# A two-layer transformer block on one core: the first stage with a joined mask, an fp32 projection and a key-only norm, and a low part that moves to GpSimd

## What is computed

```python
def _layernorm(x, axis=-1, eps=1e-05):
    m = jnp.mean(x, axis=axis, keepdims=True)
    v = jnp.var(x, axis=axis, keepdims=True)
    return (x - m) / jnp.sqrt(v + eps)
...
        qkv = x @ Wqkv.T + bqkv
        q, k, v = jnp.split(qkv, 3, axis=-1)
        q = rmsnorm(q, gq)
        k = rmsnorm(k, gk)
...
        q = apply_rope(q, cos, sin)
        k = apply_rope(k, cos, sin)
        qf = jax.nn.relu(q)
        kf = jax.nn.relu(k)
        vpad = jnp.concatenate([v, jnp.ones_like(v[..., :1])], axis=-1)
        vk = jnp.einsum('bhlp,bhld->bhpd', vpad, kf)
        res = jnp.einsum('bhpd,bhld->bhlp', vk, qf)
        attn = res[..., :-1] / (res[..., -1:] + EPS_LIN)
...
    x = L0_attn_x
    xn = _layernorm(x, axis=-1)
    x = x + _L0_attn_ref(xn, ...) + _L0_ffn_ref(xn, ...)
    xn = _layernorm(x, axis=-1)
    x = x + _L1_attn_ref(xn, ...) + _L1_ffn_ref(xn, ...)
```

## Time and profile before

| | |
|---|---|
| median of 3 runs | 414.53 us (414.43 to 414.73) |
| the profiled execution | 415.73 us, its span 413.9 us, mean granted TensorE clock 0.942 |
| VectorE busy | 361.8 us, 87% of the span |
| TensorE busy | 323.3 us, 78% |
| GpSimd busy | 235.4 us, 57% |
| ScalarE busy | 187.9 us, 45% |
| VectorE in the full step from 98.90 to 115.58 us | 15.42 of 16.68 us |
| TensorE, ScalarE, GpSimd in that step | 14.02, 11.67, 8.27 us |

### The profile page before, as it was taken

The page is one execution under the profiler, slowest core; times in us unless marked ns, Lnnn a source line. Parts: engine busy times, 40 slices in busy tenths (PEclk is TensorE's granted clock), DMA queues, the critical chain, the costliest instruction groups (busy, mean ns, idle before and its releaser), DMA issues.

```text
span 413.9 us, 5058 instructions
## 1 busy us (share of the span) xinstructions
PE 323.3 (78%) x1487; PEld 244.7 (59%) x1487; DVE 361.8 (87%) x815; ACT 187.9 (45%) x502; POOL 235.4 (57%) x149
## 2 busy tenths in 40 slices
PE   0357595887888877632409999999999999999995
PEld 0247485876777766621306666666666666666662
DVE  3786988999989975589999989999999999999791
ACT  2434546667766674630304262533526253352621
POOL 9061563634725522156345977879597787958450
PEclk9999888999999999695857999999999999999999
DMA  7720000101101002121000000000000000000000
GB/s 181 230 51 1 2 0 0 53 2 52 51 2 51 30 22 98 63 71 30 1 0 1 2 0 25 2 24 1 2 25 1 26 2 25 1 2 26 0 27 26
DMA packets 13248, 12.51 MB, mean 30 GB/s; under 512 B 1548, under 2 KB 9924, under 8 KB 13220
## 3 DMA queue, kind: packets, MB, share of 16 engines
q1 hardware_dynamic: 10944, 10.10, 7.7%
q0 software_dynamic: 736, 0.95, 1.1%
q10 hardware_dynamic: 1540, 1.12, 0.9%
HBM read 5.88 MB, written 2.10 MB: 19 GB/s over the span
## 4 chain that ended last, share of the span: by engine, by line
PE 42%; DVE 34%; issue 8%; POOL 6%; ACT 6%; DMA 1%; ACTq 1%; DVEq 0%; POOLq 0%
PE VK L840 14%; PE Q L840 12%; PE T L840 8%; PE ND L840 4%; ACT xn L555 4%; DVE mv L1105 3%; POOL prod_qk L780 3%; PE T L836 3%; DVE bst L1095 2%; POOL prod_pv L790 2%; DVE rope_a L1266 2%; DVE rope_b L1268 2%; PE Q L836 2%; DMA wout<-in_woutT 1%; DVE sgc L1466 1%
## 5 line engine op out<-in xcount | busy, mean ns | idle before, releaser
L790 POOL TENSOR_TENSOR prod_pv<-prob,qkv 128x1024 f32<-128x1024 f32 x32 | 69.6, 2212 | 45.0 <-DVE att L1383 24.2
L694 ACT ACTIVATE sg<-Q 128x512 f32<-128x512 f32 x72 | 43.1, 598 | 97.6 <-PE Q L840 94.9
L780 POOL TENSOR_TENSOR prod_qk<-qkv 128x1024 f32<-128x1024 f32 x32 | 75.9, 2402 | 16.7 <-DVE scr L1366 16.7
L840 PE MATMUL VK<-hid,w 128*128 128x512 f32 x144 | 74.5, 599 | 0.0
L840 PE MATMUL Q<-xT_hi,w_hi 128*128 128x512 f32 x72 | 52.3, 726 | 0.7 <-ACT combT L680 0.7
L1466 DVE TENSOR_TENSOR sgc<-ND,sg 128x512 f32<-128x512 f32 x64 | 43.7, 682 | 6.6 <-PE ND L840 4.6
L1479 DVE TENSOR_TENSOR hid<-T,sgc 128x512 f32<-128x512 f32 x64 | 43.6, 681 | 0.3
L840 PE MATMUL T<-xT_hi,w_hi 128*128 128x512 f32 x72 | 28.9, 401 | 17.1 <-DVE hid L1479 17.1
L743 POOL TENSOR_TENSOR mxy<-xn,amax 128x512 f32<-128x512 f32 x8 | 8.5, 1066 | 57.5 <-DVE amax L1250 57.5
L1366 DVE TENSOR_REDUCE scr<-prod_qk 128x128 f32<-128x1024 f32 x32 | 38.4, 1207 | 0.0
L1383 DVE TENSOR_REDUCE att<-prod_pv 128x128 f32<-128x1024 f32 x32 | 38.3, 1197 | 0.0
(11 more groups left out here) (202 smaller groups left out, 840.7 us busy)
## 6 DMA issues: line engine op xcount, KB each, us to landing
xT_hi<-xTs_hi SPq DMA_DIRECT2D x8, 256.0 KB, 2.3
xT_lo<-xTs_lo SPq DMA_DIRECT2D x8, 256.0 KB, 2.3
out_x<-fin SPq DMA_DIRECT2D x8, 256.0 KB, 2.3
x<-in_x SPq DMA_DIRECT2D x2, 256.0 KB, 5.0
wraw<-in_w1T SPq DMA_DIRECT2D x1, 512.0 KB, 10.8
w<-in_w2T SPq DMA_DIRECT2D x1, 512.0 KB, 5.1
wraw<-in_w3T ACTq DMA_DIRECT2D x1, 512.0 KB, 3.2
sel<-in_c_sel POOLq DMA_DIRECT2D x4, 128.0 KB, 2.8
```

Source lines behind the costliest of these rows:

```text
L694: act.activation(sg[:, side(half, s), :], QB[side(half, s)][:, :], ACT.Silu).then_inc(sg_ready, 1)
L780: pool.tensor_tensor(prod_qk[:, t % 2], bc(qkv2[:, TH * half + t, j, 0:D], 1, NB), qkv2[:, :, j, D:2 * D], ALU.mult).then_inc(qk_prod, 1)
L790: pool.tensor_tensor(prod_pv[:, t % 2].rearrange("p (h e) b -> p b h e", e=HD), bc(prob[:, t], 3, HD), qkv2[:, :, j, 2 * D:QKV].rearrange( ...
L840: return pe.matmul(o, lhsT, rhs, start=start, stop=stop)
```

## The change

It does eight things in the first part. (1) `v_ext` gets 16 columns of ones in place of one, and `headmask` and `headsel` become one mask of 144 columns, so that one product makes `vk_bd`. (2) The first projection is one fp32 product per tile; the hi and lo parts of the weights and of xnT are gone. (3) `features` scales and clips k alone (`kf`); q is transposed as it comes out of the rotary sum, and ScalarE's copy out of the bank is a relu. (4) As q is then without its norm's factor, `attention` adds the epsilon times the root in the denominator. (5) `ln_values` uses `bn_aggr` on each tile, and one addition of the epsilon. (6) ScalarE copies the second transposed tile twice, whole (`xTs`) and from there rounded (`xTs_hi`). (7) The low part of it is subtracted by GpSimd, between `mx_round` and `rope_add`. (8) `rope_add` also waits until the transposes of the chunk before have read `rope_ab`.

```diff
-            act.dma_start(headmask[:, :], d["c_headmask"]).then_inc(ld_const, 16)
-            act.dma_start(headsel[:, :], d["c_headsel"]).then_inc(ld_const, 16)
+            act.dma_start(headmask[:, 0:D], d["c_headmask"]).then_inc(ld_const, 16)
+            act.dma_start(headmask[:, D:D + H], d["c_headsel"]).then_inc(ld_const, 16)
...
-                act.activation(wqkv_hi[:, :], wqkv_raw[:, :], ACT.Copy).then_inc(wqkv_hi_ready, 1)
...
             def qfT_evac(c):
-                evac(qfT[:, :, :], tiles(T1), (qfT_ps, c + 1), [], qfT_ready)
+                act.wait_ge(qfT_ps, c + 1)
+                act.activation(qfT[:, :, :], tiles(T1), ACT.Relu).then_inc(qfT_ready, 1)
...
-                evac(xTs_hi[:, :, :], tiles(T1), (xn2T_ps, c + 1), [(xTs_free, c + 1)], xn2T_hi)
+                evac(xTs[:, :, :], tiles(T1), (xn2T_ps, c + 1), [(xn2T_lo, c)], xn2T_whole)
+                act.wait_ge(xn2T_whole, c + 1)
+                act.wait_ge(xTs_free, c + 1)
+                act.activation(xTs_hi[:, :, :], xTs[:, :, :], ACT.Copy).then_inc(xn2T_hi, 1)
...
             def rope_add(c):
                 pool.wait_ge(qkv_rope, NJ * c + NJ)
                 after(pool, feat_ready, c)
+                after(pool, qfT_ps, c)
...
+            def xn2T_lo_part(c):
+                pool.wait_ge(xn2T_hi, c + 1)
+                pool.tensor_tensor(xTs_lo[:, :, :], xTs[:, :, :], f32(xTs_hi[:, :, :]), ALU.subtract)\
+                    .then_inc(xn2T_lo, 1)
...
                 run(i, 1, mx_round)
+                run(i, 4, xn2T_lo_part)
                 run(i, 1, rope_add)
...
-                    t = mm(VK[:, 0:D + 1], qkf[:, j, 1, :], v_ext[:, j, :], j == 0, j == NJ - 1)
+                    t = mm(VK[:, 0:D + H], kf[:, j, :], v_ext[:, j, :], j == 0, j == NJ - 1)
...
                     mm(q[:, 0:QKV], ones2[:, :], bias_qkv, True, False)
-                    mm(q[:, 0:QKV], xnT_hi[:, j, :], wqkv_hi[:, :], False, False)
-                    mm(q[:, 0:QKV], xnT_hi[:, j, :], wqkv_lo[:, :], False, False)
-                    mm(q[:, 0:QKV], xnT_lo[:, j, :], wqkv_hi[:, :], False, True).then_inc(qkv_ps, 1)
+                    mm(q[:, 0:QKV], xnT[:, j, :], wqkv[:, :], False, True).then_inc(qkv_ps, 1)
...
-                V.tensor_tensor(mv[:, 0], me, mo, ALU.add)
-                V.tensor_tensor(mv[:, 1], me, mo, ALU.subtract)
-                V.tensor_tensor(mv[:, 2], qe, qo, ALU.add).then_inc(ln_value, 1)
+                for k in range(2):
+                    for j in range(NJ):
+                        t = V.bn_aggr(mv[:, k, j, :], bst[:, k, j, :])
+                t.then_inc(ln_value, 1)
                 dve.wait_ge(ln_value, LNV * i + 1)
...
+                V.tensor_scalar(root[:, 0, 0:2 * NJ].rearrange("p (n j) -> p n j", j=NJ), mv[:, :, :, 1], LN_EPS,
+                                None, ALU.add).then_inc(ln_value, 1)
...
-            def xnT_lo_part(c):
-                dve.wait_ge(xnT_hi_ready, c + 1)
-                V.tensor_tensor(xnT_lo[:, :, :], tiles(T0), f32(xnT_hi[:, :, :]), ALU.subtract)\
-                    .then_inc(xnT_lo_ready, 1)
...
-                V.scalar_tensor_tensor(qkf[:, :, :, :].rearrange("p j n f -> p (j n) f"),
-                                       rope_ab[:, :, :, :].rearrange("p j n f -> p (j n) f"), 0.0,
-                                       bc(root[:, 4, 2 * NJ:4 * NJ], 2, D), ALU.max, ALU.mult)\
+                V.scalar_tensor_tensor(kf[:, :, :], rope_ab[:, :, 1, :], 0.0,
+                                       bc(qk_norms(4)[:, :, 1], 2, D), ALU.max, ALU.mult)\
                     .then_inc(feat_ready, 1)
...
-                V.tensor_tensor(vk_bd[:, 0:D], VK[:, 0:D], headmask[:, :], ALU.mult)
-                V.tensor_scalar(vk_bd[:, D:D + H], headsel[:, :], VK[:, D:D + 1], None, ALU.mult)\
-                    .then_inc(vk_ready, 1)
+                V.tensor_tensor(vk_bd[:, :], VK[:, 0:D + H], headmask[:, :], ALU.mult).then_inc(vk_ready, 1)
...
-                run(i, 4, xn2T_lo_part)
                 run(i, 1, rope_tile(2))
```

More of the change, by code:

```diff
@@ L120, in build @@
         rope_s = sba("rope_s", [P, NJ, 2, D])
-        wqkv_raw = sba("wqkv_raw", [P, QKV])
-        wqkv_hi = sba("wqkv_hi", [P, QKV], F32R)
-        wqkv_lo = sba("wqkv_lo", [P, QKV], F32R)
+        wqkv = sba("wqkv", [P, QKV])
         rope_a = sba("rope_a", [P, NJ, 2 * D])
@@ L188, in build @@
         xTs_lo = sba("xTs_lo", [P, NJ, P], F32R)
+        xTs = sba("xTs", [P, NJ, P])
         T0, T1, Q0, Q1, VK, ND0, ND1, Q2 = (
@@ L275, in build @@
         xn2T_ps = sem("xn2T_ps")
+        xn2T_whole = sem("xn2T_whole")
         xn2T_hi = sem("xn2T_hi")
@@ L447, in _ @@
             sp.dma_start(x[:, 0], xv[:, 0]).then_inc(ld_x[0], 16)
-            sp.dma_start(wqkv_raw[:, :], d["wqkvT"]).then_inc(ld_w0, 16)
+            sp.dma_start(wqkv[:, :], d["wqkvT"]).then_inc(ld_w0, 16)
             sp.dma_start(rope_c[:, :, 0, :], d["c_cos"]).then_inc(ld_rope, 16)
@@ L565, in xn2_tiles, with xnT_evac @@
                 return lambda c: normalise_tiles(xn2, x[:, c], 1, (2 * half, 2 * half + 1)).then_inc(xn2_ready, 1)
-            def xnT_hi_evac(c):
-                evac(xnT_hi[:, :, :], tiles(T0), (xnT_ps, c + 1), [], xnT_hi_ready)
+            def xnT_evac(c):
+                evac(xnT[:, :, :], tiles(T0), (xnT_ps, c + 1), [], xnT_ready)
             def xdT_evac(c):
@@ L622, in step @@
                 run(i, 2, xdT_evac)
-                run(i, 1, xnT_hi_evac)
+                run(i, 1, xnT_evac)
                 run(i, 2, qfT_evac)
@@ L1136, in rsqrt @@
                 dve.wait_ge(rsqrt_step, at + 4)
-                V.scalar_tensor_tensor(shift[:, :, :].rearrange("p n j -> p (n j)"),
-                                       mv[:, 0].rearrange("p n j -> p (n j)"), -0.5, root[:, 4, 0:2 * NJ],
+                V.scalar_tensor_tensor(shift[:, :, :], mv[:, :, :, 0], -1.0,
+                                       root[:, 4, 0:2 * NJ].rearrange("p (n j) -> p n j", j=NJ),
                                        ALU.mult, ALU.mult).then_inc(rsqrt_step, 1)
@@ L1311, in plus_ffn @@
                 V.tensor_tensor(l0_sum[:, :, :], l0_sum[:, :, :], tiles(ND1), ALU.add).then_inc(l0_ready, 1)
-            def xn2T_lo_part(c):
-                dve.wait_ge(xn2T_hi, c + 1)
-                V.tensor_tensor(xTs_lo[:, :, :], tiles(T1), f32(xTs_hi[:, :, :]), ALU.subtract)\
-                    .then_inc(xn2T_lo, 1)
             def step(i):
@@ L1333, in step @@
                 run(i, 1, mx_maxima)
-                if not at(i, 1):
-                    run(i, 1, xnT_lo_part)
                 run(i, 1, mx_scales)
```

51 lines of the change are left out of this document (18 added, 33 removed).

## The result

The changed kernel takes 429.40 us (median of 4 runs, 427.88 to 430.23) against 414.63 us for the kernel before beside it. The ratio is 1.0351, with a 95% interval of 1.0321 to 1.0381: 3.5% slower, 14.8 us. The profiled execution has a span of 427.6 us, 13.7 more than the 413.9 of before.

What follows compares the result with a forecast made beforehand. VectorE, 15.42 of a full step's 16.68 us busy, partly standing still behind GpSimd, was read as the bound. Step terms of +8.1 and clock +4.0 make +12.1 on 414.53: 426.6 us, own range 423.8 to 430, wider 418 to 432.

Steps and rivals of the forecast that it cites:

- GpSimd's low part and TensorE's queue: Full steps 5 to 8: low part queues behind GpSimd's rounding, output product behind TensorE's wait for it; +1.0 us each.
- The clock: Steps 4 to 8: TensorE's 2.6 us wait drops its clock in half of the five steps, 1.6 us each; +4.0 us.
- the layer-1 tile and the output product: TensorE behind the wait: these two (0.84 + 1.06) take up to twice as long at lower clock; 1.6 us taken.
- Clock stays down: Rival: TensorE's lower clock lasts into the next step's transposes, value product and tile 0, 1.8 us more; 431 to 440, chance 0.13.
- Step 4: First step with the low part, TensorE on its lower clock until tile 0: 18.8 us, +1.85.
- Steps 1 to 3: Steps without low part: rotary sum holds VectorE at the end, fewer moment operations, step 1 gains 0.9; together -1.45 us.
- Step 9: No rounding here, but the layer-1 tile waits for two ScalarE copies and GpSimd; +1.1 us.
- Steps 10 and 11 and what follows: TensorE's wait in step 10 grows by 1.3 us in full, step 11 repeats it; +2.6 us.
- The parts that VectorE gives up: Some 3 us per full step leave VectorE, but all that it saves becomes waiting.
- The addition is not held: Rival: GpSimd's rotary sum does not hold VectorE's new addition, steps 1 to 3 gain 4 us more; 418.6, chance 0.07.
- VectorE still sets the end: Rival: VectorE decides the step's end, -1.4 us a step over eight steps; 403.5, chance 0.06.
- The two halves cancel: Rival: low part behind the rounding costs half, the early steps give 3 us; 414.5, chance 0.04.

Runs made afterwards that it cites:

- the filled wait: The changed kernel with eleven unused 512-column TensorE products ahead of the first layer-1 tile in steps 4 to 8; 423.39 us, ratio 1.0193.
- the half-filled one: The changed kernel with five unused 512-column TensorE products ahead of the first layer-1 tile in steps 4 to 8; 423.09 us, ratio 1.0206.

## Why the prediction was right

I forecast 426.6 us and a range of 418 to 432; it is 429.4. The mechanism was the one forecast, and the sum was 2.8 us short. The total is closer than its terms: steps 1 to 3 gained 1.75 us more than I gave, and that hid half of the 3.3 us by which I had steps 4 to 9 too short. That is luck. And whether the clock falls in two, three or more of the steps I had no way to tell; half was a guess. Step by step, against the span of the profiled execution:

- **GpSimd's low part and TensorE's queue: right, and close in size.** In step 8, the one at full clock, the low part ended 13.95 us behind the root (13.9 forecast), the wait was 2.44 (2.6), the step 17.88 (17.7). The term was +1.0 a step and measured +1.2.
- **The clock: right in kind, wrong in its parts, low in size.** I let half of five steps lose it at 1.6 us, +4.0. It fell in three of the five. Steps 5 to 7 together took 5.4 us more than three of 17.88, and the filled wait gave back some 6.5. The step that was mis-sized is "the layer-1 tile and the output product". I had the clock falling at once, at the layer-1 tile, and it fell 0.9 to 1.4 us later, so its own step paid less than 1.6. From the end of the wait to the next root, steps 4, 5 and 7 took 4.63, 4.64 and 5.10 us for the 3.93 of step 8: 0.7 to 1.2 more. What I left out of the sum are the products at the head of the next step, which I had put into the rival "Clock stays down" at 1.8. In steps 5 and 6 the wait ended 15.91 and 15.62 behind the root for 13.95, so two of the three falls cost 1.7 to 2.0 there. The measured course is a mixture of the forecast and that rival.
- **Step 4: +1.85 forecast, +1.05 measured.** I had TensorE on its lower clock until tile 0, as before. In this execution it was not, and the mxm operations ended 8.26 behind the root instead of the 9.8 forecast; the clock fell later in the step. In the filled wait and the half-filled one, whose program is the same up to there, that stretch was at the lower level, and step 4 took 19.85 and 18.98. So this term differs from execution to execution.
- **Steps 1 to 3: -1.45 forecast, -3.2 measured.** The step that failed is that the rotary sum on GpSimd "holds VectorE at the step's end". In step 1 the additions came ahead of the rotary sum, and the sum then held the second operation of the next step (1.58 us). That moved the hold over the root: step 1 is 3.2 shorter, step 2 0.8 longer. In step 2 TensorE's granted clock was 0.81, for 1.00 before, so a part of the 0.8 may be the clock's; the two were not separated.

```profile
26.50 0.37 DVE L1111 TENSOR_SCALAR root<-mv 128x8 f32<-128x8 f32 x1
26.78 0.16 DVE L1117 TENSOR_SCALAR root<-ss 128x12 f32<-128x12 f32 x1
...
26.80 2.35 POOL L758 TENSOR_TENSOR rope_ab<-rope_a,rope_b 128x1024 f32<-128x1024 f32 x1
27.60 1.58 DVE L1126 TENSOR_TENSOR root<-root 128x20 f32<-128x20 f32 x1
```

- **Step 9: +1.1 forecast, +3.0 measured.** The mechanism's part is about 1.4: the half-filled run, with its clock up in this step, took 16.54 for 15.15. The other 1.6 is the clock, which I had let fall in steps 4 to 8 only:

```profile
166.57 0.66 PE L840 MATMUL T<-ident,attn 128*128 128x128 f32 x4 [1.14 <-DVE attn L1286]
168.12 0.45 PE L844 MATMUL Q<-bias,ones 128*128 128x400 f32 x1 [0.90 <-POOL xTs_lo L763]
169.21 1.91 PE L844 MATMUL ND<-wout,attnT 128*128 128x128 f32 x8
```

  The filled wait has the same two waits in step 9, 1.14 and 0.90 us, and there this product took 1.05. So this fall is not explained by the waits next to it, and why it came is open.

- **Steps 10 and 11 and what follows: +2.6 forecast, +2.6 measured** (-0.46, +2.03 and +1.0). TensorE's wait in step 10 grew as forecast, from 1.41 to 2.70 us. But I had placed half of the 2.6 in that step's length, and it arrived later. What the 1.0 behind the routing consists of was not followed, so the agreement of the sum shows little.
- **The parts that VectorE gives up: hidden, as forecast.** The aggregates took 0.64 for eight (0.65), the fp32 tiles followed each other at 0.82 (0.83), and the addition was held. The rival "The addition is not held" falls with the 2.31 us row.
- **The rival "VectorE still sets the end"** gave 403.5 and a step 1.4 shorter. Where the low part stays on VectorE, this is what happens: the steps are 1.1 to 1.5 shorter and the time 406.8 to 408.2. Its terms without that low part were 0.7 for the mask and 0.4 for the moments, less 0.3 for the tiles. Measured, the mask and the key-only norm took 0.65 off a full step, the aggregates 0.75, both together 1.47, so these two add up. The fp32 projection took 0.67 off on the kernel before, but cost 0.4 on top of the other two: it and the joined mask remove the same stall, VectorE's 0.89 us behind GpSimd.
- **The rival "The two halves cancel"** doesn't come to its 414.5. Half of the 9.55 us of steps 4 to 11 less 3 is +1.8, so 416.3; nothing else hangs on it.

## What to carry to other kernels

Moving work from the busiest engine to an idler one costs when the idler one hands over later: ask where in the receiver's queue the work comes to stand, and who waits for the result with what queued behind. Here 1.3 us on GpSimd in the wrong place cost 5% where the same subtraction on VectorE took 0.6 us, and the same instruction two places earlier in the queue gave half of it back. A wait on TensorE can be priced twice, by its length and by the clock that it may cost for what follows; filling a part of it with unused products is a cheap way to tell the two apart. Gains that remove the same stall don't add: measure each alone and all together.

## What the runs showed of the hardware

- Behind waits of 2.44 to 2.70 us TensorE's granted clock fell in some steps and not in others of the same program, 0.9 to 1.4 us after work had begun again. In the kernel before with the low part on GpSimd, one fell during such a wait. With 1.29 to 1.52 us left of the same wait it stayed at 1.00 in steps 5 to 8. One fall, in step 9, came behind waits of 1.14 and 0.90 us that did no harm in another run.
- The hold of VectorE by GpSimd moves with the order in which the two begin. It fell on the epsilon addition (2.31 us), on the rms addition (1.27) or on a tensor_tensor of the next step (1.58), always to the end of the rotary sum. The aggregates were not held, also where they ran beside that sum (0.64 for eight, in the run with the aggregates alone).
- TensorE's unused products of 512 columns ran at some 0.25 us each, and steps 6 to 8 were the same length with five of them as with eleven.
